# Experts that gather their rows by a table of tokens, in place of a scatter into slots

## The chip, the cores and the metric

The kernel runs on one core of one Trainium2 chip. The time is device time in microseconds of one execution; the kernel before has a median of 3042.47 us. The program is one launch with all of a small decoder in it, and the change touches two of its stages.

## The reference, cut to what matters

The part around the change is a layer with a mixture of experts: 2048 tokens (four batches of 512) of 512 numbers, normalized; a classifier into 64, of which 32 are real experts and 32 are empty; the best 8 for each token; each real expert takes its tokens, at most 256.

```python
logits = xf @ w_cls.T
scores = jax.nn.softmax(logits, axis=-1)
_, topk_idx = jax.lax.top_k(scores + bias[None, :], K)        # K = 8 of 64
w = jnp.take_along_axis(scores, topk_idx, axis=-1)
w = w / (w.sum(-1, keepdims=True) + EPS) * SCALE
...
buf = jnp.zeros((E, CAP, H), xf.dtype).at[ids_s, pos].set(x_exp[order], mode='drop')   # 32 x 256 x 512
gu = jnp.einsum('ech,ehf->ecf', buf, w_gate_up)
g, u = jnp.split(gu, 2, axis=-1)
act = jax.nn.silu(g) * u
y = jnp.einsum('eci,eih->ech', act, w_down)
```

`buf` is what the change is about: the rows of each expert, in the order of the tokens (place `pos`), with zeros behind the last.

## The kernel before

The decoder runs in stages, each a function with one program for each engine: attention, `graph_and_router` (names gr_), `experts` (ex_), further attention layers (at_), and a last network (ff_). Between two stages all engines meet at a barrier.

`graph_and_router` works through four batches b. For each, thresholds of a 512x512 matrix are found: ACT and DVE count how many entries are above a test value, POOL works out the next test value (`update(b, r, j)`, L2235 and L2236, in rounds r), and round 8 makes a table of powers of two (L2232). DVE meanwhile strikes out maxima (`strike_out`), builds the adjacency (L2072), adds it to x, normalizes the rows (`normalize`, L2089, which needs `rstds(b, 1)` of POOL, L2240) and does the `router` of the batch: softmax, best 8, `hot` (a one for each choice, L2144), `mask` (L2147), gate weights, and the place of each choice in its expert, which comes from PE's running counts and the sum so far, `taken` (L2172). PE also has "asides": weights of the last network that it turns and mixes, and `late_units`, 16 weight tiles for the attention, of which DVE writes low parts and copies at the end of the stage (L2201, L2204).

The rows of the experts lie in DRAM, in `slot_rows`, 8192 slots of 2 KB. SP zeroes them at the start (L1711, 16 transfers of 1 MB). POOL then sends each token's row to its slots: `scatter(b, lo, hi)` issues indirect DMAs (L2248), one for each tile of 128 tokens and each of the 8 choices, 32 a batch. Their places in POOL's program are written out by hand: those of batches 0 and 1 lie between the rounds of later batches (`EARLY`, `LATE`), those of batches 2 and 3 behind the last round.

`experts` goes through 32 experts with two buffers for everything (u = e % 2). SP loads the 256 rows of an expert (L2353, 512 KB) as soon as PE has turned those of two experts before; PE turns them (L2408), then gate and up, then down of the expert before (L59 to L61: each product is three, of high and low parts). ACT makes the high parts, DVE the low ones (L2493), and POOL the low part of the down weights, `split_d` (L2538), which waits for ACT's high part (L2464). SP loads the weights of the next but one (L2358, L2359). PE's order is turn(k), gate_up(k-1), down(k-2), turn(k+1).

## Time and profile before

| what | us |
|---|---|
| median of 3 runs | 3042.47 |
| lowest and highest | 3036.84, 3046.91 |
| the profiled execution, its own time | 3039.41 |
| its span in the profile | 3037.4 |
| busy in the span: PE, DVE, ACT, POOL | 2468.5, 1837.5, 1242.0, 855.3 |
| graph_and_router | about 668 to 1162 |
| experts | 1162 to about 1471 |

All times in the profile count from the start of the span. A row of the timeline has the start, the duration, the engine, the line, the operation and tiles, and in brackets how long the engine had been idle and what it waited for. "issue" is idle time for which the profile shows no releaser. "DMA to landing" counts from the start of the issuing instruction. The granted clock is a share of 2.4 GHz.

### The profile page before, as it was taken

How to read it: one execution, taken by the hardware profiler on the slowest of the kernel's cores; microseconds unless marked ns; L12 is line 12 of the kernel's file. 1: busy time of each engine (PE TensorE's matmuls, PEld its weight loads, DVE VectorE, ACT ScalarE, POOL GpSimd, SP SyncE). 2: the span in 40 equal slices, each digit the busy share in tenths (PEclk: the TensorE clock that was granted, in tenths of full speed). 3: DMA queues.
4: the chain of work that ended last, by engine and by line, in shares of the span. 5: the costliest groups of instructions: out<-in, count | busy, mean ns of one | idle time of the engine just before them, and what ended most of it. 6: DMA issues, size and time to landing. Idle time of an engine off the chain costs nothing. (4 is left out here: it accounts for less than half of the span.)

```text
span 3037.4 us, 34907 instructions
## 1 busy us (share of the span) xinstructions
PE 2468.5 (81%) x12662; PEld 1636.9 (54%) x12662; DVE 1837.5 (60%) x2917; ACT 1242.0 (41%) x1873; POOL 855.3 (28%) x1198
## 2 busy tenths in 40 slices
PE   5898989863443356999448999999999869999999
PEld 4454545321221135999334554545555538888887
DVE  3766576627888964777557777565655544444443
ACT  2444444328656624666203433344333323333332
POOL 2232222215578773333443332001211110000000
PEclk8999999976665677999768999999999979999999
DMA  3213131227122245999585656333433323101000
GB/s 117 64 43 84 43 84 46 70 77 287 62 97 92 84 161 180 305 304 303 173 182 138 157 147 156 88 89 100 113 95 92 102 85 133 42 1 42 1 28 14
DMA packets 200952, 340.40 MB, mean 112 GB/s; under 512 B 28809, under 2 KB 60425, under 8 KB 198754
## 3 DMA queue, kind: packets, MB, share of 16 engines
q1 hardware_dynamic: 177250, 299.80, 32.5%
q0 software_dynamic: 20480, 37.87, 5.1%
q8 instruction: 86, 1.41, 0.2%
q10 hardware_dynamic: 3072, 0.79, 0.1%
q14 instruction: 64, 0.52, 0.1%
HBM read 182.30 MB, written 109.05 MB: 96 GB/s over the span
## 5 line engine op out<-in xcount | busy, mean ns | idle before, releaser
L757 DVE TENSOR_REDUCE at_negmax<-at_ps 128x2 f32<-128x1024 f32 (+3 forms) x256 | 259.1, 1016 | 120.7 <-PE at_ps L523 63.7
L670 ACT ACTIVATE at_probs<-at_ps 128x1024 f32<-128x1024 f32 (+3 forms) x256 | 221.7, 866 | 269.9 <-PE at_ps L538 267.6
L1367 DVE TENSOR_REDUCE a_negmax<-a_ps 128x2 f32<-128x1024 f32 x128 | 155.1, 1217 | 137.0 <-PE a_ps L1120 136.4
L1896 ACT ACTIVATE gr_act_signs<-gr_signed,gr_test 128x512 bf16<-128x512 f32 x248 | 177.2, 716 | 81.5 <-POOL gr_test L2236 53.4
L59 PE MATMUL ff_ps<-ff_xnT_hi,ff_s_hi 128*128 128x512 f32 x512 | 201.1, 393 | 5.1 <-DVE ff_xnT_lo L2766 5.1
L61 PE MATMUL ff_ps<-ff_xnT_hi,ff_s_lo 128*128 128x512 f32 x512 | 200.4, 391 | 0.0
L60 PE MATMUL ff_ps<-ff_xnT_lo,ff_s_hi 128*128 128x512 f32 x512 | 200.4, 391 | 0.0
L538 PE MATMUL at_ps<-at_qk 98*128 98x512 f32 (+3 forms) x512 | 172.1, 418 | 21.2 <-DMA at_qk<-at_mrow 11.5
L2796 DVE TENSOR_TENSOR ff_hid<-ff_hid,ff_ps 128x512 f32<-128x512 f32 x64 | 44.0, 688 | 238.6 <-ACT ff_hid L2741 238.6
L1268 ACT ACTIVATE a_probs<-a_ps 128x1024 f32<-128x1024 f32 x128 | 130.9, 1023 | 135.1 <-PE a_ps L1138 134.6
L518 PE MATMUL at_ps<-at_qk 96*128 96x512 f32 (+3 forms) x512 | 162.4, 381 | 19.5 <-DVE at_xnT_lo L818 8.9
L538 PEld LDWEIGHTS at_ps<-at_qk 98*128 98x128 f32 x512 | 83.2, 194 | 163.2 <-issue 91.9
L2741 ACT ACTIVATE ff_hid<-ff_ps 128x512 f32<-128x512 f32 x64 | 38.3, 598 | 303.4 <-PE ff_ps L61 303.4
L2538 POOL TENSOR_TENSOR ex_d_lo<-first_d,ex_d_hi 128x1024 fp32r<-128x1024 f32 x32 | 95.9, 2996 | 216.1 <-ACT ex_d_hi L2464 216.1
L59 PE MATMUL ex_ps<-ex_x_hi,ex_gu_hi 128*128 128x256 f32 x512 | 148.0, 289 | 0.0
L2248 POOL DMA_INDIRECT slot_rows<-shared_x,slots x128 | 135.6, 1060 | 40.1 <-issue 40.1
L60 PE MATMUL ex_ps<-ex_x_lo,ex_gu_hi 128*128 128x256 f32 x512 | 145.3, 284 | 0.0
L61 PE MATMUL ex_ps<-ex_x_hi,ex_gu_lo 128*128 128x256 f32 x512 | 145.3, 284 | 0.0
L852 POOL TENSOR_SCALAR_AFFINE_SELECT at_probs<-at_probs 128x256 f32<-128x256 f32 x128 | 52.4, 410 | 292.1 <-ACT at_probs L670 292.1
L782 DVE RECIPROCAL at_weighed<-at_weighed 128x128 f32<-128x128 f32 x128 | 119.8, 940 | 15.1 <-ACT at_weighed L705 15.1
L726 ACT CAST at_part<-at_ps 128x512 fp32r<-128x512 f32 x64 | 37.4, 587 | 215.8 <-PE at_ps L61 204.2
L873 POOL TENSOR_TENSOR at_oT<-at_weighed 128x512 f32<-128x512 f32 x32 | 40.7, 1272 | 298.0 <-DVE at_weighed L782 298.0
(410 smaller groups left out, 6557.1 us busy)
## 6 DMA issues: line engine op xcount, KB each, us to landing
at_qk<-at_part SPq DMA_DIRECT2D x384, 128.0 KB, 2.5
first_gu<-in_L_ffn_w_gate_up_dram SPq DMA_DIRECT2D x32, 1024.0 KB, 5.6
a_qk<-a_part SPq DMA_DIRECT2D x192, 128.0 KB, 2.3
slot_rows<-gr_zeros SPq DMA_DIRECT2D x16, 1024.0 KB
first_d<-in_L_ffn_w_down_dram SPq DMA_DIRECT2D x32, 512.0 KB, 6.5
ex_rows<-slot_rows SPq DMA_DIRECT2D x32, 512.0 KB, 4.6
out_rows<-ex_y SPq DMA_DIRECT2D x32, 512.0 KB, 3.1
gr_aside_raw<-in_L_ffn_W_dram SPq DMA_DIRECT2D x48, 256.0 KB, 3.1
```

Source lines behind the costliest of these rows:

```text
L59: pe.matmul(out, lh, rh, start=start, stop=False, skip_group_check=True)
L60: pe.matmul(out, lh, rl, start=False, stop=False, skip_group_check=True)
L61: return pe.matmul(out, ll, rh, start=False, stop=stop, skip_group_check=True)
L518: mm = pe.matmul(bank(key, i, 0, n), qk[0:KROWS, g % STACKS, 0, j, t * P:(t + 1) * P], qk[0:KROWS, g % STACKS, 1, j, 0:n], start=True, sto ...
L538: mm = pe.matmul(bank(key, i, lo), qk[0:KROWS + 2, g % STACKS, 1, j, t * P:(t + 1) * P], qk[0:KROWS + 2, g % STACKS, 0, j, lo:S], start=Tr ...
L670: act.activation(probs[:, t % 2, 2 * w:2 * w + 2, lo:S], banks(("kq", g, s), lo), ACT.Exp, scale=SCALE).then_inc(free(("kq", g, s)), 1)
L757: dve.reduce_max(negmax[:, g % 2, :].rearrange("p (j t) -> p j t", t=NT)[:, 2 * w:2 * w + 2, t], banks(("qk", g, s), 0, width(g, t)), AX.X ...
L782: dve.reciprocal(weighed[:, 1, t * P:(t + 1) * P], weighed[:, 1, t * P:(t + 1) * P]).then_inc(rec_done, 1)
L1268: act.activation(probs[:, t % 2, 2 * w:2 * w + 2, :], banks(("kq", g, s)), ACT.Exp, scale=SCALE).then_inc(free(("kq", g, s)), 1)
L1367: dve.reduce_max(negmax[:, g % 2, :].rearrange("p (j t) -> p j t", t=NT)[:, 2 * w:2 * w + 2, t], banks(("qk", g, s)), AX.X, negate=True).t ...
L1896: act.activation(act_signs[:, j, :], src, ACT.Sign, scale=-1.0, bias=against, accum_out=total[:, i, j:j + 1]).then_inc(counted_to[j], 1)
L2248: pool.indirect_dma_start(slot_rows, bass.IndirectOffsetOnAxis(slots[:, n:n + 1], 0), xn[:, b % 2, at // TOPK, :], None, bounds_check=SLOT ...
```

## The change

Nothing is scattered and nothing is zeroed but one row. DVE's normalized rows go to DRAM as they are (`normed`, 2049 rows, row 0 all zeros), by one direct DMA of SP for each batch. What is computed is, for each slot, the number of its token (0 for an empty slot): the table `index`, 128 x 64.

The table is made by PE from products of ones. A place from 0 to 255 is taken apart by DVE into a block (of 8) and a row in it (of 32) (`places`). DVE writes `rows_hot`, a one at the row, by one comparison 128x4096 for each batch (`write_rows`). POOL writes `block_hot`, the token's number in its tile and the tile's number at the block (`blocks_hot`, ten operations). PE multiplies the two, 32 matmuls a batch, summed over the 128 tokens (`table`); DVE adds each batch to `found` (`add_table`). At the end `sum_tokens` joins the two numbers, 16 small matmuls move them to the partitions (`move_tokens`) and `keep_index` writes them as integers.

In `experts` SP's row load is gone. POOL gathers: two indirect DMAs of 128 rows for each expert (`gather`). `hot` is bf16 now, and the sum for the gate weights is made in two halves. `rstds(b-1, 1)` of POOL stands behind round 7 for every batch (it was 8 for batch 1 and 5 for the others).

```diff
+        rows_hot, block_hot = sb("rows_hot", [P, NT, E_ROUTED, ROW], BF16), sb("block_hot", [P, 2, NT, E_ROUTED, BLOCKS], BF16)
...
-            many = slot_rows.rearrange("(p q r) d -> q p (r d)", p=P, r=zeros.shape[1] // D)
-            for q in range(ZERO_DMAS):
-                sp.dma_start(many[q], zeros[:]).then_inc(zeroed, 16)
-            sp.dma_start(none_row, zeros[0:1, 0:D]).then_inc(zeroed, 16)
+            for dst in (none_row, normed[0:1, :]):
+                sp.dma_start(dst, zeros[0:1, 0:D]).then_inc(zeroed, 16)
+            normed_tiles = normed[1:T + 1, :].rearrange("(b t p) d -> b p t d", p=P, t=NT)
+
+            def store_normed(b):
+                sp.wait_ge(xn_done, NT * (b + 1))
+                sp.dma_start(normed_tiles[b], xn[:, b % 2]).then_inc(normed_out, 16)
...
+            def table(b):
+                pe.wait_ge(logT_copied, b + 1)
+                pe.wait_ge(blocks_set, b + 1)
+                pe.wait_ge(vector_rows, b + 1)
+                for t in range(NT):
+                    for g in range(GROUPS):
+                        e = SIDE * g
+                        mm = pe.matmul(ps[:, LOGT, g * P // 2:(g + 1) * P // 2], rows_hot[:, t, e:e + SIDE, :].rearrange("p e r -> p (e r)"),
+                                       block_hot[:, :, t, e:e + SIDE, :], start=t + g == 0, stop=t == NT - 1 and g == GROUPS - 1, skip_group_check=True)
+                mm.then_inc(tabled, 1)
+
+            def move_tokens():
+                pe.wait_ge(index_step, 1)
+                by_side = token_of[:].rearrange("p g (t w) -> p w g t", w=SIDE)
+                for h in range(SIDE):
+                    for w in range(SIDE):
+                        mm = pe.matmul(ps[ROW * w:ROW * (w + 1), MOVED, h * GROUPS * HALVES:(h + 1) * GROUPS * HALVES], env.ident[:, ROW * h:ROW * (h + 1)],
+                                       by_side[:, w], start=True, stop=True, skip_group_check=True)
+                mm.then_inc(moved, 1)
...
                 choices(b)
                 run_asides(b + 1)
+                if b + 1 < B:
+                    table(b)
             for u, (j, c) in enumerate(late_units):
+                if u == len(LATE_BANKS):
+                    table(B - 1)
+                    move_tokens()
...
             def normalize(b):
                 dve.wait_ge(rstd_done[1], b + 1)
                 if b >= 2:
-                    dve.wait_ge(scattered[b % 2], 16 * NT * TOPK * (b // 2))
+                    dve.wait_ge(normed_out, 16 * (b - 1))
                 for t in range(NT):
                     dve.tensor_scalar(xn[:, b % 2, t, :], xo[:, t, :], mv[:, 1, t, 0:1], rstd[:, 1, t, 0:1],
                                       ALU.subtract, ALU.mult).then_inc(xn_done, 1)
+
+            def add_table(b):
+                dve.wait_ge(tabled, b + 1)
+                for h in range(SIDE):
+                    here = slice(ROW * h, ROW * (h + 1))
+                    new = ps[here, LOGT, :].rearrange("p (g n h k) -> p h g n k", n=2, h=SIDE, k=BLOCKS)[:, h]
+                    if b:
+                        dve.tensor_tensor(found[here], found[here], new, ALU.add).then_inc(tab_added, 1)
+                    else:
+                        dve.tensor_copy(found[here], new).then_inc(tab_added, 1)
 
             def finish(b):
                 exact_bounds(b)
                 adjacency(b)
                 blend_x(b)
+                if b:
+                    add_table(b - 1)
...
                 def gate_weights():
-                    for t in range(NT):
-                        step(dve.tensor_tensor(prod[:, t], hot[:, t], bcast_mid(score[:, t, :], TOPK), ALU.mult), wait=t == NT - 1)
-                    step(dve.reduce_sum(k8[:, 0, :], prod[:].rearrange("p t k e -> p (t k) e"), AX.X))
+                    for u in range(2):
+                        for i in range(2):
+                            t = 2 * u + i
+                            step(dve.tensor_tensor(prod[:, i], hot[:, t], bcast_mid(score[:, t, :], TOPK), ALU.mult), wait=i == 1)
+                        step(dve.reduce_sum(k8[:, 0, 2 * u * TOPK:2 * (u + 1) * TOPK], prod[:].rearrange("p t k e -> p (t k) e"), AX.X))
...
+                def places():
                     dve.wait_ge(counted, b + 1)
                     step(dve.tensor_tensor(place[:], counts[:, 0:NT * E_ROUTED].rearrange("p (t e) -> p t e", e=E_ROUTED),
                                            bcast_mid(taken[:], NT), ALU.add))
                     step(dve.tensor_tensor(taken[:], taken[:], counts[:, NT * E_ROUTED:(NT + 1) * E_ROUTED], ALU.add))
+                    if b:
+                        dve.wait_ge(blocks_set, b)
+                    flat, chosen = place[:].rearrange("p t e -> p (t e)"), mask[:].rearrange("p t e -> p (t e)")
+                    dve.tensor_scalar(row[:], flat, 1.0 / ROW, 0.5 / ROW - 0.5, ALU.mult, ALU.add).then_inc(decoding, 1)
+                    dve.wait_ge(decoding, DECODE * b + 1)
+                    dve.tensor_scalar(block_of[:], row[:], 1.5 * 2.0 ** 23, 1.5 * 2.0 ** 23, ALU.add, ALU.subtract).then_inc(decoding, 1)
+                    dve.wait_ge(decoding, DECODE * b + 2)
+                    dve.scalar_tensor_tensor(out=row[:], in0=block_of[:], scalar=-float(ROW), in1=flat, op0=ALU.mult, op1=ALU.add).then_inc(decoding, 1)
+                    dve.wait_ge(decoding, DECODE * b + 3)
+                    dve.scalar_tensor_tensor(out=row[:], in0=row[:], scalar=1.0, in1=chosen, op0=ALU.add, op1=ALU.mult).then_inc(decoding, 1)
...
+            def write_rows(b):
+                dve.wait_ge(decoding, DECODE * (b + 1))
+                dve.wait_ge(numbers_set, 1)
+                if b:
+                    dve.wait_ge(tabled, b)
+                dve.tensor_tensor(rows_hot[:].rearrange("p t e r -> p (t e) r"), bcast_mid(row_iota[:], NT * E_ROUTED),
+                                  bcast_last(row[:], NT * E_ROUTED, ROW), ALU.is_equal).then_inc(vector_rows, 1)
+
+            def sum_tokens():
+                add_table(B - 1)
+                dve.wait_ge(tab_added, SIDE * B)
+                dve.scalar_tensor_tensor(out=token_of[:], in0=found[:, :, 1, :], scalar=float(P), in1=found[:, :, 0, :], op0=ALU.mult, op1=ALU.add
+                                         ).then_inc(index_step, 1)
+
+            def keep_index():
+                dve.wait_ge(moved, 1)
+                dve.tensor_copy(index[:], ps[:, MOVED, 0:SLOTS // P]).then_inc(index_kept, 1)
 
             strike_out(0, 0, ROUNDS + 1)
             for b in range(B):
                 finish(b)
             for u, (j, c) in enumerate(late_units):
                 high, low = late_jobs[j][1:]
+                if u == len(LATE_BANKS):
+                    sum_tokens()
+                if u == 2 * len(LATE_BANKS):
+                    keep_index()
...
-            def scatter(b, lo, hi):
-                for at in range(lo, hi):
-                    if at == 0:
-                        pool.wait_ge(slots_done, 2 * b + 1)
-                        pool.tensor_tensor(pool_carrier[:, b:b + 1], env.minus_half[:, 0:1], env.minus_half[:, 0:1], ALU.mult)
-                    n = b * NT * TOPK + at
-                    pool.indirect_dma_start(slot_rows, bass.IndirectOffsetOnAxis(slots[:, n:n + 1], 0), xn[:, b % 2, at // TOPK, :], None,
-                                            bounds_check=SLOTS - 1, oob_is_err=False).then_inc(scattered[b % 2], 16)
+            def blocks_hot(b):
+                pool.wait_ge(decoding, DECODE * (b + 1))
+                if b:
+                    pool.wait_ge(tabled, b)
+                for n in range(BLOCKS):
+                    pool.tensor_scalar(in_block.rearrange("p (e k) -> p e k", k=BLOCKS)[:, :, n], block_of[:], float(n), None, ALU.is_equal).then_inc(numbers, 1)
+                pool.wait_ge(numbers, (BLOCKS + 1) * b + BLOCKS)
+                pool.tensor_tensor(block_hot[:, 1].rearrange("p t e k -> p t (e k)"), in_block.rearrange("p (t m) -> p t m", t=NT),
+                                   bcast_last(tile_no[:, NT * b:NT * (b + 1)], NT, E_ROUTED * BLOCKS), ALU.mult).then_inc(numbers, 1)
+                pool.wait_ge(numbers, (BLOCKS + 1) * (b + 1))
+                pool.tensor_scalar(in_block, in_block, token[:, 0:1], None, ALU.mult).then_inc(blocks_set, 1)
...
-            LATE = 22
-            EARLY = {0: 2, 4: 5, 5: 1, 7: 1, 9: 3, 10: 1, 11: 2, 13: 2, 15: 1, 17: 1, 18: 1, 20: 1, 21: 1}
-            assert sum(EARLY.values()) + TESTS - LATE == NT * TOPK
             for b in range(B):
-                sent = TESTS - LATE
                 for r in range(TESTS):
                     for j in range(COUNTED[b]):
                         update(b, r, j)
-                    if b and r == (8 if b == 1 else 5):
+                    if b and r == 7:
                         rstds(b - 1, 1)
-                    if b >= 2 and r in EARLY:
-                        scatter(b - 2, sent, sent + EARLY[r])
-                        sent += EARLY[r]
-                    if 0 < b < B - 1 and r >= LATE:
-                        if b == 1 and r == LATE:
-                            pool.wait_ge(zeroed, 16 * (ZERO_DMAS + 1))
-                        scatter(b - 1, r - LATE, r - LATE + 1)
+                if b:
+                    blocks_hot(b - 1)
                 rstds(b, 0)
-            scatter(B - 2, 0, 12)
             rstds(B - 1, 1)
-            scatter(B - 2, 12, NT * TOPK)
-            scatter(B - 1, 0, NT * TOPK)
-            for i in range(2):
-                pool.wait_ge(scattered[i], 16 * NT * TOPK * B // 2)
-
+            blocks_hot(B - 1)
...
-                turned[u].wait(sp, i, 0)
-                sp.dma_start(rows[:, u], rows_dram[bass.ds(e, 1)].rearrange("e p t d -> (e p) t d")).then_inc(rows_in[u].sem, 16)
...
+            def gather(e):
+                i, u = e // 2, e % 2
+                turned[u].wait(pool, i, 0)
+                for t in range(CT):
+                    at = CT * (E_ROUTED // SIDE * (e % SIDE) + e // SIDE) + t
+                    pool.indirect_dma_start(rows[:, u, t, :], None, normed, bass.IndirectOffsetOnAxis(index[:, at:at + 1], 0)).then_inc(rows_in[u].sem, 16)
+
+            gather(0)
+            gather(1)
             split_d(0, 0)
             split_d(0, 1)
+            gather(2)
             for e in range(E_ROUTED):
+                if e + 3 < E_ROUTED:
+                    gather(e + 3)
                 if e + 2 < E_ROUTED:
                     split_d(e // 2 + 1, e % 2)
```

The order of the instructions shows three places. The names of semaphores in brackets are those of an earlier stage that had the same numbers; the sentences say what they stand for here.

POOL at the end of the graph stage, before. The last rounds are behind it; a0_norm_done stands for the slots of a batch, a0_feat_done and a0_kf_ready for DVE's statistics.

```order
L2240 TENSOR_TENSOR gr_rstd<-gr_mv,minus_half 128x4 [waits a0_feat_done]
L2246 TENSOR_TENSOR gr_pool_carrier<-minus_half 128x1 [waits a0_norm_done]
L2248 DMA slot_rows<-shared_x,slots 8192x512 x12
L2240 TENSOR_TENSOR gr_rstd<-gr_mv,minus_half 128x4 [waits a0_kf_ready]
L2248 DMA slot_rows<-shared_x,slots 8192x512 x20
L2246 TENSOR_TENSOR gr_pool_carrier<-minus_half 128x1 [waits a0_norm_done]
L2248 DMA slot_rows<-shared_x,slots 8192x512 x32
```

The same place now: a0_y_ready stands for the decoded places of the batch.

```order
L2349 TENSOR_SCALAR gr_block_hot<-gr_block_of 128x128 x7
L2351 TENSOR_TENSOR gr_block_hot<-gr_block_hot,gr_tile_no 128x1024 [waits gr_numbers]
L2354 TENSOR_SCALAR gr_block_hot<-gr_block_hot,gr_token 128x1024 [waits gr_numbers]
L2342 TENSOR_TENSOR gr_rstd<-gr_mv,minus_half 128x4 [waits a0_feat_done]
L2342 TENSOR_TENSOR gr_rstd<-gr_mv,minus_half 128x4 [waits a0_kf_ready]
L2349 TENSOR_SCALAR gr_block_hot<-gr_block_of 128x128 [waits gr_tabled,a0_y_ready]
```

The 64 scatters that stood here are gone, and each batch's ten operations stand in front of a rstd of the next, or last.

POOL in the experts, before: only the splits, each waiting for ACT's high part (a0_ones_set for the even experts, a0_rows_set for the odd).

```order
L2538 TENSOR_TENSOR ex_d_lo<-first_d,ex_d_hi 128x1024 [waits a0_ones_set]
L2538 TENSOR_TENSOR ex_d_lo<-first_d,ex_d_hi 128x1024 [waits a0_rows_set]
L2538 TENSOR_TENSOR ex_d_lo<-first_d,ex_d_hi 128x1024 [waits a0_ones_set]
L2538 TENSOR_TENSOR ex_d_lo<-first_d,ex_d_hi 128x1024 [waits a0_rows_set]
L2538 TENSOR_TENSOR ex_d_lo<-first_d,ex_d_hi 128x1024 [waits a0_ones_set]
```

And now, from the split of expert 0 on (a0_xT_hi and a0_p_ready stand for PE's turn of the even and the odd experts).

```order
L2634 TENSOR_TENSOR ex_d_lo<-first_d,ex_d_hi 128x1024 [waits a0_ones_set]
L2634 TENSOR_TENSOR ex_d_lo<-first_d,ex_d_hi 128x1024 [waits a0_rows_set]
L2644 DMA ex_rows<-normed,index 128x512 [waits a0_xT_hi]
L2644 DMA ex_rows<-normed,index 128x512
L2644 DMA ex_rows<-normed,index 128x512 [waits a0_p_ready]
L2644 DMA ex_rows<-normed,index 128x512
L2634 TENSOR_TENSOR ex_d_lo<-first_d,ex_d_hi 128x1024 [waits a0_ones_set]
L2644 DMA ex_rows<-normed,index 128x512 [waits a0_xT_hi]
L2644 DMA ex_rows<-normed,index 128x512
L2634 TENSOR_TENSOR ex_d_lo<-first_d,ex_d_hi 128x1024 [waits a0_rows_set]
```

From gather(4) on the order is split, gather, split, gather: split_d(j) stands in front of gather(j+2).

DVE at the end of the graph stage, now. Before, the late weights (L2204 and L2201 of before) followed each other here; a0_sums_out is DVE's own last result.

```order
L2269 TENSOR_TENSOR weights<-gr_k 128x32 [waits a0_sums_out]
L2306 TENSOR_TENSOR at_wq_lo<-gr_ps,at_wq_hi 128x512 [waits gr_late_high] x4
L2147 TENSOR_TENSOR gr_found<-gr_found,gr_ps 32x128 [waits gr_tabled]
L2147 TENSOR_TENSOR gr_found<-gr_found,gr_ps 32x128 x3
L2284 SCALAR_TENSOR_TENSOR gr_token_of<-gr_found 128x64 [waits gr_tab_added]
L2306 TENSOR_TENSOR at_wk_lo<-gr_ps,at_wk_hi 128x512 [waits gr_late_high] x4
L2289 CAST index<-gr_ps 128x64 [waits gr_moved]
L2306 TENSOR_TENSOR at_wv_lo<-gr_ps,at_wv_hi 128x512 [waits gr_late_high] x4
L2303 COPY at_wo<-gr_ps 128x512 [waits gr_late_turned] x4
```

The additions wait for PE's last table, and the index for PE's moves, with the late weights of three more matrices queued behind.

## Rows read from the trace of the kernel before

**Rows 1.** windows of three stretches: us, busy time, granted clock, DMA share

```profile
core 0: us, PE busy (x) PEld busy (x) DVE busy (x) ACT busy (x) POOL busy (x), PEclk, DMA share, GB/s
668.00:1067.00 399.00, 150.31 (x500) 82.87 (x501) 330.71 (x963) 255.76 (x638) 260.61 (x645) 0.64 0.37 129
1067.00:1162.00 95.00, 39.12 (x188) 26.49 (x186) 45.13 (x112) 17.45 (x31) 67.78 (x68) 0.68 0.39 128
1200.00:1440.00 240.00, 238.42 (x1725) 223.16 (x1724) 179.04 (x153) 156.78 (x166) 75.18 (x26) 1.00 0.90 302
```

**Rows 2.** timeline at the boundary: start us, duration, engine, line, wait

```profile
1067.57 1.10 POOL L2248 DMA_INDIRECT slot_rows<-shared_x,slots  x1 [0.17 <-issue]
...
1153.63 0.97 POOL L2248 DMA_INDIRECT slot_rows<-shared_x,slots  x1 [0.30 <-issue]
1124.90 2.47 DVE L2201 COPY at_wo<-gr_ps 128x512 f32<-128x512 f32 x4
1161.97 0.88 SPq L2353 DMA_DIRECT2D ex_rows<-slot_rows  x2
1165.53 1.97 PE L2408 MATMUL ex_ps<-ident,ex_rows 128*128 128x128 f32 x8 [39.84 <-DMA ex_rows<-slot_rows]
```

**Rows 3.** timeline of DVE in the graph stage, rows with a wait

```profile
792.27 1.92 DVE L2089 TENSOR_SCALAR shared_x<-shared_rows,gr_mv,gr_rstd 128x512 f32<-128x512 f32 x4 [7.98 <-POOL gr_rstd L2240]
906.63 0.42 DVE L2126 TENSOR_REDUCE gr_r<-gr_ps 128x4 f32<-128x256 f32 x1 [2.21 <-PE gr_ps L1794]
967.00 0.74 DVE L2051 TENSOR_SCALAR_CACHE_REDUCE gr_dve_flags<-gr_signed,gr_test 128x512 bf16<-128x512 f32 x1 [4.84 <-POOL gr_test L2236]
1017.04 0.42 DVE L2130 TENSOR_REDUCE gr_r<-gr_expd 128x4 f32<-128x256 f32 x1 [2.60 <-ACT gr_expd L1909]
```

**Rows 4.** timeline of SP, PE and POOL, early in the graph stage

```profile
676.11 17.62 SPq L1711 DMA_DIRECT2D slot_rows<-gr_zeros  x14
723.42 1.09 PE L1823 MATMUL gr_ps<-ident,gr_aside_raw 128*128 128x128 f32 x4 [5.43 <-DMA gr_aside_raw<-in_L_ffn_W_dram]
788.60 0.29 POOL L2229 TENSOR_SCALAR gr_half<-gr_total,gr_offset 128x1 f32<-128x1 f32 x1 [0.19 <-ACT gr_act_signs L1896]
791.19 1.05 POOL L2240 TENSOR_TENSOR gr_rstd<-gr_mv,minus_half 128x4 f32<-128x4 f32 x1
```

**Rows 5.** groups of 668 to 1162, each shape apart

```profile
L2144 DVE TENSOR_TENSOR gr_hot<-gr_iota,gr_choice 128x2048 f32<-128x2048 f32 x4 | 9.2, 2294 | 0.1
L2147 DVE TENSOR_REDUCE gr_mask<-gr_hot 128x128 bf16<-128x1024 f32 x4 | 7.6, 1888 | 0.1
L2172 DVE TENSOR_TENSOR gr_place<-gr_ps,gr_taken 128x128 f32<-128x128 f32 x4 | 1.2, 291 | 0.6 <-PE gr_ps L1806 0.5
L2232 POOL TENSOR_SCALAR gr_steps<-gr_powers,gr_base 128x23 f32<-128x23 f32 x8 | 3.0, 380 | 0.0
```

**Rows 6.** timeline of POOL and DVE at 815 us

```profile
815.12 2.38 POOL L2235 TENSOR_SCALAR gr_half<-gr_total,gr_offset 128x1 f32<-128x1 f32 x1
815.05 2.29 DVE L2144 TENSOR_TENSOR gr_hot<-gr_iota,gr_choice 128x2048 f32<-128x2048 f32 x1
```

**Rows 7.** timeline of one period of the experts

```profile
1301.07 1.03 PE L2408 MATMUL ex_ps<-ident,ex_rows 128*128 128x128 f32 x8
1310.45 1.03 PE L2408 MATMUL ex_ps<-ident,ex_rows 128*128 128x128 f32 x8
1302.39 2.97 POOL L2538 TENSOR_TENSOR ex_d_lo<-first_d,ex_d_hi 128x1024 fp32r<-128x1024 f32 x1 [6.41 <-ACT ex_d_hi L2464]
1307.09 2.29 DVE L2493 TENSOR_TENSOR ex_gu_lo<-first_gu,ex_gu_hi 128x2048 fp32r<-128x2048 f32 x1
```

**Rows 8.** operations of L270, the gathers of the attention

```profile
L270 POOL DMA_INDIRECT shared_rows<-out_rows,slots x102: 940/964/1474, 1524.7 to 1871.2; - x102
DMA to landing us min/median/max: 3.8/5.4/9.4
```

**Rows 9.** operations of L2353, the experts' row loads, 1180 to 1450

```profile
DMA to landing us min/median/max: 4.3/4.7/8.0
```

85 lines of the change are left out of this document (59 added, 26 removed).

## The prediction, made before the changed kernel had run

> **What bounds the kernel now.** I read the windows by stage first [rows 1]. The graph stage (668 to 1162 us) has PE busy for only 189 of 494 us, DVE for 331 of 399 us before 1067 us; this stage waits for DVE and the engines that hand it numbers. In the experts (1200 to 1440) PE is busy 238.42 of 240 us at full clock, the DMA engines 0.90 of the time: nothing there is free on PE's side, and whatever makes PE wait is paid in full. Then the boundary between the two, engine by engine [rows 2]. DVE ends its last late weight at 1124.90 + 2.47 = 1127.4. POOL goes on issuing scatters, 64 of them from 1067.57 to 1153.63, one in (1153.63 - 1067.57) / 63 = 1.37 us, and SP starts the experts' first load at 1161.97, 34.6 us after DVE was done. So POOL's queue of scatters sets this boundary. Third, DVE's own waits inside the stage [rows 3]: on POOL's rstd (7.98) and test (4.84), on PE's logits (2.21) and ACT's exponentials (2.60).
>
> **The change, part by part.** The sum is made against the profiled execution (3039.41 us, span 3037.4).
>
> Zeroing slot_rows goes. SP issues it from 676.11 for 17.6 us and more [rows 4], 16 MB through the engines that the first asides need: PE waits 5.43 us there for a raw tile [rows 4]. The loop runs 1.5 to 2 us late by it at DVE. **-1.7**. For batch 1, rstds(0, 1) moves from behind round 8 of POOL's loop to behind round 7. Round 8 is the costly one, with the powers: from 788.60 to the rstd at 791.19 [rows 4], 2.6 us. DVE waits 7.98 us for this rstd [rows 3], so it gains **-2.7**. For batches 2 and 3 it moves from round 5 to 7. A round of the rest of the loop takes 2 to 3 us; these batches' normalize then waits longer for POOL, by my reading of the rounds in all **+3.1** (bounds: 0, if POOL is ahead by then, and two rounds for each, +10).
>
> VectorE's work per batch. places() is four operations 128x128; the nearest row is the one that adds `taken`, 291 ns [rows 5], so with gaps 1.3 us. write_rows compares 128x4096; the same comparison at 128x2048 takes 2294 ns [rows 5], so 4.4 to 4.6. The output is bf16 and no longer f32; I take no gain for it (at half the time it would be 2.3 and the routers 9 us shorter together). Splitting the sum over `prod` in two adds 0.3. Together 6.0 to 6.1 in every router. The bf16 `hot` may make the mask's sum (1888 ns [rows 5]) shorter; I take 0.25 a batch, 1.0 in all.
>
> What of that shows. Batch 0: all, **+6.1**. Batch 1: the router's waits for PE (2.21) and ACT (2.60), and then the one for POOL's test (4.84) [rows 3], come from queues that this DVE work doesn't move, so a later DVE waits less, and the batch gains what POOL, without scatters between its rounds, is earlier: 6.0 - 9.7 = **-3.7**. Batch 2: the first two kinds alone, at about the same size, 6.0 - 4.6 = **+1.4**. The bound on the other side is that those waits move along with DVE: 9.7 + 4.6 more. add_table, four copies from PSUM over 32 partitions, 0.25 to 0.3 each: **+1.1** once; the others lie in a wait. Up to the last adjacency: -1.7 - 2.7 + 3.1 + 6.1 - 3.7 + 1.1 + 1.4 = **+3.6**; with the mask's gain +2.6.
>
> POOL in the stage. It loses 128 scatters (1.37 us of its queue each, above) and gains blocks_hot four times: eight 128x128 operations and two of 128x1024. The nearest POOL rows are 380 ns for 128x23 [rows 5] and 2.97 for 128x1024 with two SBUF inputs [rows 7]; with one it should be under that, so 8 x 0.3 + 2 x 2.5 = 7.4 us. It stands behind the rounds, and then the next rstds(b, 0) and PE's table. As POOL idles for ACT there, 7.4 is mostly cover; if the cover is gone, three times 3 us are paid, which I keep for the range. PE's 32 table matmuls a batch stand behind its asides, in a stage in which PE is idle more than half of the time [rows 1]; I cost them at nothing.
>
> The end of the stage. After: DVE ends at 1127.4 + 6.1 (last router) + 1.5 (add_table, token_of) + 3.5 to 4 (it must see POOL's last blocks_hot, the last table and the 16 f32 moves) + 0.3 (index) = 1139.0 to 1139.4. Between the last work of the stage and SP's first issue of the next lies the engines' barrier: after the last scatter's end, 1154.60, it was 7.4 us with that scatter's landing [rows 2]. Here nothing is in the air, and I take 1.2 (bounds 0 and 7.4). So the experts begin at 1140.6, not 1161.97: **-21.2**. Ahead of the experts: 2.6 - 21.2 = **-18.6**.
>
> Experts, first one. From SP's issue to PE's turn there were 1161.97 to 1165.53 [rows 2], 3.6. Now POOL issues two gathers and the second must land: 1.27 + 5.4 = 6.7. **+3**.
>
> Experts, steady. Here the order matters: POOL does split_d(j), gather(j+2), split_d(j+1), gather(j+3). One turn at 1301.07, next at 1310.45, 9.38 later [rows 7]. POOL's split_d runs from 1302.39 to 1305.36 [rows 7], 4.29 behind the turn, and it is split_d(14) behind turn 15; so gather(16) stands behind it and has to have landed by turn 16. Gathers take 0.96 us each [rows 8], and "issue", 0.3, stands between two DMAs of POOL [rows 2]: the second is issued from 5.87 to 6.84 behind the turn, and 9.38 - 5.87 = 3.5 us are left for landing (measured from the start of the issue). Before, SP's load was free from 1.4 on, with 8 us left for a 4.7 landing [rows 9]. The gathers that the trace has, of the same shape from DRAM to SBUF in the attention, land in 3.8 / 5.4 / 9.4 (least, median, most) [rows 8]: more than 3.5 even at the least. POOL waits for ACT's copy of the weights, and that for PE's down ahead of the turn; so a late turn isn't passed on by one expert but by two. With period p and landing L: 2p = 5.87 + 9.38 + L, and PE stalls (L - 3.5) / 2 per expert. L = 3.8 gives 0.15, 5.4 gives 0.95, 6.5 gives 1.5.
>
> To that comes DVE. While it runs a large operation with two SBUF inputs POOL's own doesn't proceed: an operation of 0.35 us took 2.38 beside the 2.29 of L2144, and ended with it [rows 6]. The experts' gu_lo is such an operation, from 1307.09 for 2.29 us [rows 7], 6.02 behind the turn, right on the second gather. In the other parity it starts 1.3 later. So the second gather ends up to 1.5 us later in half of the experts: on average 0.6 of chain, 0.3 of stall. Stall 0.95 + 0.3 = 1.25 us, for 29 experts **+36**.
>
> The Trainium skill has a rule for the lock (SBUF — State Buffer: the port pair that DVE and GpSimd share is held for a full instruction by a DVE operation with two SBUF inputs, against a GpSimd one that reads SBUF). The trace agrees, by the 2.38 us above. By that page alone every second gather that meets gu_lo would wait for its end, at 8.31 behind the turn.
>
> Sum: -18.6 + 3 + 36 = **+20** on 3039.4, 3060. The median of the runs shown is 3042.5, 3 above the profiled one; I give **3062**. Costed at nothing: store_normed, four direct stores of 1 MB in place of 32 MB of scatters, under a DMA share of 0.37 [rows 1]; if one were in the way it would be by some 3 us.
>
> **Rivals.**
> (a) No stall: faster. The gathers land within 3.5 us, or POOL gets ahead of PE. Then -18.6 + 3 = -15.6: 3025 to 3030. It decides from a landing of 3.9, where 29 x 0.2 eats 6 of the 15.6 and 9 are left. For it: the scatters were a cheap transfer, issued every 1.37 us with no wait but "issue" [rows 2]. Against it: no gather of the trace landed under 3.8, and in the experts other transfers hold the engines for 0.90 of the time [rows 1].
> The Trainium skill speaks for this one (DMA: Bandwidth & Descriptors, on the anatomy of a software-generated DMA): 2.0 us plus the bytes at 436 GB/s, an estimate of 2.6 us for 256 KB. By that there would be no stall and 3027. The trace disagrees with it, 3.8 at the least and 5.4 in the median.
> (b) A heavy stall: the gathers share the engines with 1.5 MB of weights, which SP issues as split_d ends, so at the same moment. The upper part of the spread, 6.5 to 9.4, would give 1.5 to 2.9, with gu_lo 1.8 to 3.2: +52 to +90, so 3078 to 3115. For it: the share of 0.90, and the simultaneous issue. Against it: the rows load of today is as large, in the same share, and landed in 4.7 [rows 9].
> (c) They cancel: landing 4 to 5, stall 0.2 to 0.85 with the lock, 3033 to 3052.
> (d) The graph stage gives nothing: blocks_hot or the table isn't covered and the last one delays the index by 7 us more; PE's granted clock, 0.64 to 0.68 on the mean of this stage [rows 1], between its levels of 0.5 (1.2 GHz) and 1.0 (2.4 GHz), stays longer on the lower one. That adds 5 to 15 to any of the others.
>
> **How the numbers follow.** My forecast, a stall of 0.9 to 1.6, has 0.42 (own range 3050 to 3078). (a) 0.17, (b) 0.16, (c) 0.25, with (d) spread over them. Low end: between (a) and (c) 3028; high: the landing of 7 with the lock, 3092. That leaves about 0.1 on each side. 0.3%, 9.1 us, is what a measurement of this kernel can tell from no change: faster is (a) and a little of (c), 0.2; same most of (c), 0.2; slower 0.6.
>
> **What would show it.** In the profile after: the first gather near 1141; nothing named slot_rows; DVE's comparison 128x4096 near 4.5 us; PE's turn in the experts with a wait on the rows' DMA of about 1.2 us each, and a period of 10.6 and not 9.38; the gathers' landing median near 5.4; PE's clock still full in the experts; ends of the second gather stretched beside gu_lo. Wrong would be: turns without a wait (then (a)); a first gather after 1150 (then (d)); or waits that PE shows on d_lo in place of the rows, which would say that POOL's queue itself, and not the landing, is late.

## The result and the profile after

The changed kernel takes 3102.07 us in the median (3097.72 to 3104.90, 4 runs), the kernel before 3041.34 beside it (3036.84 to 3046.91, 4 runs): a ratio of 1.0198, with a 95% interval of 1.0176 to 1.0219. It is slower by about 60 us, where 20 were forecast, and outside the range (3028 to 3092). The profiled execution has 3097.72 us, 58.3 more than that of before.

The windows of the changed kernel, with the boundary of the stages where it lies now, answer to [rows 1].

```profile
core 0: us, PE busy (x) PEld busy (x) DVE busy (x) ACT busy (x) POOL busy (x), PEclk, DMA share, GB/s
668.00:1067.00 399.00, 157.03 (x576) 88.97 (x576) 344.04 (x974) 257.95 (x642) 237.97 (x614) 0.61 0.28 90
1067.00:1146.00 79.00, 38.02 (x270) 28.97 (x270) 60.14 (x144) 14.41 (x26) 21.47 (x13) 0.74 0.39 142
1200.00:1440.00 240.00, 206.31 (x1371) 192.56 (x1371) 141.94 (x121) 124.21 (x130) 99.64 (x60) 0.93 0.70 239
```

In the experts PE is busy 206 of 240 us, where it was 238, and the mean clock is 0.93 and not 1.00. The DMA share fell from 0.90 to 0.70: the engines had less to do in the same time, so they are no bound by themselves. A stage that was full has got holes.

Cut at the same places in both profiles, the time went like this. The stage starts at DVE's first instruction of it, 668.92 before and 672.65 after.

| piece | before | after | difference | forecast |
|---|---|---|---|---|
| start of the graph stage to the adjacency of batch 3 | 401.4 | 402.7 | +1.3 | +2.6 |
| from there to the first issue of the experts' rows | 91.6 | 71.0 | -20.6 | -21.2 |
| issue to the first turn of PE | 3.6 | 5.4 | +1.9 | +3 |
| first turn to the 32nd | 287.4 | 363.4 | +76.0 | +36 |
| all that the change doesn't touch (ahead of and behind it) | 2253.4 | 2253.4 | 0 | 0 |

The 0 of the last row hides two differences of the same size: the stage starts 3.7 us later, and the time behind the last turn is 3.8 us shorter (1580.7 us and not 1584.5). They cancel by chance, and nothing here says why they differ. The row "start of the graph stage to the adjacency" rests on one profile of each kernel. Of the nine other profiles of versions that leave this stretch alone six have 402.4 to 402.7 us there, and three 405.0 to 405.9.

One term is wrong, by 40 us. The boundary, in the timeline after (to be held against [rows 2]):

```profile
1111.64 11.96 POOL L2349 TENSOR_SCALAR gr_block_hot<-gr_block_of 128x128 bf16<-128x128 f32 x8 [21.66 <-DVE gr_row L2247]
1126.12 2.85 POOL L2354 TENSOR_SCALAR gr_block_hot<-gr_block_hot,gr_token 128x1024 bf16<-128x1024 bf16 x1
1129.07 1.87 PE L1855 MATMUL gr_ps<-gr_block_hot,gr_rows_hot 128*128 128x64 bf16 x32 [8.55 <-issue]
1141.69 2.47 DVE L2303 COPY at_wo<-gr_ps 128x512 f32<-128x512 f32 x4
1146.38 1.26 POOL L2644 DMA_INDIRECT ex_rows<-normed,index  x1 [17.41 <-SPq L180]
1151.82 1.97 PE L2504 MATMUL ex_ps<-ident,ex_rows 128*128 128x128 f32 x8 [9.33 <-DMA ex_rows<-normed,index]
```

POOL gathers from 1146.38 (at 1161.97 SP loaded before, in a profile that had begun the stage 3.7 us earlier). The last ones of blocks_hot run from 1111.64 to 1128.97, 17.3 us for which I had put 7.4. PE has been idle for 8.55 us when its table starts, 0.1 us behind them (the row names no releaser), but DVE's router ends only at 1129.4, so most of it was hidden.

DVE in the graph stage, timeline, against [rows 3], with the first and the last row by which the pieces were cut:

```profile
672.65 0.09 DVE L2026 MEMSET gr_taken<- 128x32 f32 x1 [3.26 <-PEq L53]
790.82 1.92 DVE L2138 TENSOR_SCALAR shared_x<-shared_rows,gr_mv,gr_rstd 128x512 f32<-128x512 f32 x4 [4.44 <-POOL gr_rstd L2342]
895.80 1.92 DVE L2138 TENSOR_SCALAR shared_x<-shared_rows,gr_mv,gr_rstd 128x512 f32<-128x512 f32 x4 [3.88 <-POOL gr_rstd L2342]
1075.34 2.49 DVE L2121 SCALAR_TENSOR_TENSOR gr_adjacent<-gr_adjacent,first_gu 128x512 f32<-128x512 f32 x4
```

And the groups of the stage, DVE and POOL, each shape apart (line, operation, shapes, count, busy us, mean ns, idle before):

```profile
L2278 DVE TENSOR_TENSOR gr_rows_hot<-gr_row_iota,gr_row 128x4096 bf16<-128x4096 f32 x4 | 17.7, 4425 | 0.1
L2187 DVE TENSOR_REDUCE gr_r<-gr_ps 128x4 f32<-128x256 f32 x4 | 1.7, 421 | 8.4 <-PE gr_ps L1816 8.2
L2191 DVE TENSOR_REDUCE gr_r<-gr_expd 128x4 f32<-128x256 f32 x4 | 1.7, 417 | 0.7 <-ACT gr_expd L1958 0.6
L2208 DVE TENSOR_REDUCE gr_mask<-gr_hot 128x128 bf16<-128x1024 bf16 x4 | 7.5, 1881 | 0.1
L2349 POOL TENSOR_SCALAR gr_block_hot<-gr_block_of 128x128 bf16<-128x128 f32 x32 | 32.1, 1153 | 22.9 <-DVE gr_row L2247 21.7
```

The wait for batch 0's rstd fell from 7.98 us [rows 3] to 4.44, and that for batch 1's rose from 2.10 to 3.88. The waits for PE's logits are 8.4 us summed over the four batches, of which 8.23 stand in the last one (8.39 before), and those for the exponentials are 0.7: the waits of batches 1 and 2 that I had expected to be eaten are eaten.

One period of two experts in the timeline, against [rows 7], and the last turn:

```profile
1228.72 1.03 PE L2504 MATMUL ex_ps<-ident,ex_rows 128*128 128x128 f32 x8
1230.04 2.97 POOL L2634 TENSOR_TENSOR ex_d_lo<-first_d,ex_d_hi 128x1024 fp32r<-128x1024 f32 x1 [9.21 <-ACT ex_d_hi L2560]
1233.16 1.24 POOL L2644 DMA_INDIRECT ex_rows<-normed,index  x1
1234.70 0.95 POOL L2644 DMA_INDIRECT ex_rows<-normed,index  x1 [0.30 <-issue]
1234.74 2.29 DVE L2589 TENSOR_TENSOR ex_gu_lo<-first_gu,ex_gu_hi 128x2048 fp32r<-128x2048 f32 x1
1241.63 1.92 PE L2504 MATMUL ex_ps<-ident,ex_rows 128*128 128x128 f32 x8 [3.38 <-DMA ex_rows<-normed,index]
1252.63 1.03 PE L2504 MATMUL ex_ps<-ident,ex_rows 128*128 128x128 f32 x8
...
1515.20 1.03 PE L2504 MATMUL ex_ps<-ident,ex_rows 128*128 128x128 f32 x8
```

The turn at 1228.72 has no wait. Behind it POOL splits, issues one gather and then the second, at 1234.70, 5.98 behind the turn. PE is done 9.5 us behind that turn and waits 3.38 us more for the rows; 1241.63 - 1234.70 = 6.9 us from the issue to PE's start. The next turn has no wait, and lies 11.00 us on, not 9.38. What the operations of L2644 (the gathers) say together:

```profile
L2644 POOL DMA_INDIRECT ex_rows<-normed,index x64: 945/950/1991, 1146.4 to 1506.4; - x64
  PE ex_ps L2504: 61.2, 16
DMA to landing us min/median/max: 3.4/6.7/8.2
```

61.2 us of waits of PE in 16 places, 9.33 of them at the very first. A landing of 6.7 in the median, where I had taken 5.4. So 51.9 of the 76.0 us are waits. The other 24 are in the turns' distance after each wait: 15 times 11.00 - 9.38 = 1.6. The windows behind the wait that ends at 1241.6, columns as above, show in what:

```profile
1241.60:1244.60 3.00, 2.97 (x14) 2.97 (x15) 1.06 (x2) 1.63 (x3) 2.54 (x3) 0.52 1.08 300
1244.60:1247.60 3.00, 3.00 (x25) 3.00 (x24) 2.39 (x2) 1.80 (x2) 0.09 (x1) 0.91 1.11 359
1247.60:1250.60 3.00, 3.00 (x25) 2.87 (x24) 1.13 (x1) 0.00 (x0) 0.00 (x0) 1.00 1.03 372
```

The granted clock is 0.52 for the first 3 us behind a wait of 3.4 us, then 0.91, then 1.00. PE is busy all through them. At 0.5 (1.2 GHz) it does half as much: (1 - 0.52) x 3 + (1 - 0.91) x 3 = 1.7 us lost.

### The profile page after: what moved, and what is told of

It reads as the page before. It is cut to its first block and busy times, and to the rows that moved or that the text cites. A ratio compares the mean times of both kernels' runs of the same rounds, so it can differ in the third digit from the quotient of the medians.

```text
span 3095.9 us, 35090 instructions
## 1 busy us (share of the span) xinstructions
PE 2499.3 (81%) x12822; PEld 1665.5 (54%) x12822; DVE 1864.9 (60%) x2959; ACT 1241.8 (40%) x1873; POOL 851.1 (27%) x1176
## 5 line engine op out<-in xcount | busy, mean ns | idle before, releaser
L59 PE MATMUL ex_ps<-ex_x_hi,ex_gu_hi 128*128 128x256 f32 x512 | 155.1, 303 | 0.0
L630 PE MATMUL at_ps<-at_wo,at_oT 128*128 128x512 f32 x256 | 115.8, 606 | 6.8 <-POOL at_oT L873 6.6
```

Source lines behind the costliest of these rows:

```text
L59: pe.matmul(out, lh, rh, start=start, stop=False, skip_group_check=True)
L630: mm = pe.matmul(bank(key, i), oT[:, dc, t * P:(t + 1) * P], woT[:, dc, :], start=dc == 0, stop=dc == NC - 1, skip_group_check=True)
```

## The experiments

**The gathers ahead of the split.** One change of order in POOL's program:

```diff
             split_d(0, 0)
-            split_d(0, 1)
             gather(2)
+            split_d(0, 1)
+            gather(3)
             for e in range(E_ROUTED):
-                if e + 3 < E_ROUTED:
-                    gather(e + 3)
+                if e + 4 < E_ROUTED:
+                    gather(e + 4)
```

> POOL's order in the experts is changed: gather(k+2) stands in front of split_d(k), so that it waits only for the turn of expert k. Theory A (the gather's place behind the split is late, and its landing of 6.7 us does not fit into the 3.5 us that are left): the gather is issued near the turn two experts ahead and has over 14 us to land, so PE's waits of 3.3 us at every other turn are gone, the period is 9.38 again, 32 turns take about 288 us and not 363, the clock is full, and the time is about 3098 - 76 = 3022. Theory B (the engines of the DMA are the limit, or gathers are slow for what goes on beside them, so that an earlier issue only makes them wait longer): turns still wait 2 to 3 us, and the time stays above 3080.

Measured: 3032.13 us (10 runs) beside 3040.73 of before, ratio 0.9972 (0.9960 to 0.9984). The landing is still slow, 7.0 us in the median and 9.9 at most, and nobody waits for it but the first turn. Theory B falls: with the same transfers beside them, gathers that are issued one expert earlier are in time. The 32 turns take 292.2 us; 288 were expected, and 3022. What the rest is shows in the windows of its experts, first and second half (columns as above):

```profile
1200.00:1317.00 117.00, 117.00 (x845) 109.95 (x844) 86.51 (x74) 75.97 (x81) 61.72 (x38) 1.00 0.89 306
1317.00:1447.00 130.00, 125.58 (x891) 115.79 (x890) 109.80 (x79) 81.06 (x86) 64.23 (x37) 1.00 0.86 289
```

In the first half PE is busy all the time, at full clock. In the second, the periods of the last 13 turns are 9.68 to 10.48 us and not 9.38, and DVE's busy time rises from 0.74 to 0.84 of the stretch, without more to do. The timeline there, POOL and DVE:

```profile
1397.71 2.40 POOL L2634 TENSOR_TENSOR ex_d_lo<-first_d,ex_d_hi 128x1024 fp32r<-128x1024 f32 x1 [4.14 <-ACT ex_d_hi L2560]
1398.30 2.89 DVE L2621 TENSOR_TENSOR shared_x<-shared_x 128x1024 f32<-128x1024 f32 x1
```

The butterfly of DVE (L2621, 128x1024, two operands in SBUF), 1.22 us in the first half, takes 2.89: it ends 1.1 us behind POOL's split, which had begun 0.6 us before it. The split is as short as it ever was (2.40). Before the change the butterfly was first, and the split, 0.5 us behind it, took 2.97 [rows 7]:

```profile
1301.87 1.22 DVE L2525 TENSOR_TENSOR shared_x<-shared_x 128x1024 f32<-128x1024 f32 x1
```

So whoever starts first of the two holds up the other. ACT had waited 2.07 us for a weight load until 1313.8, and that made DVE late once; by my reading each late butterfly (2.81 to 3.36 us, to the end) then kept DVE late for the next. When this version was run again, it went the same way: a wait of ACT for the weights until 1344.9 (2.35 us), and from the next butterfly on 2.82 to 3.36 us each.

**The rows by a direct load of SP**, with the new graph stage. The gathers are left out, and SP loads where it did before, from another array, so the experts compute on other rows.

```diff
                 e = i * 2 + u
+                turned[u].wait(sp, i, 0)
+                sp.dma_start(rows[:, u], gu_dram[bass.ds(e, 1)].rearrange("e p c f -> (e p) c f")[:, 0:CT, :]).then_inc(rows_in[u].sem, 16)
```

> No gather: SP loads 512 KB for each expert as before the change, by one direct DMA where it stood, from another array (the first half of each expert's gate and up weights), so the experts compute on other rows than the reference's. The table is made as in the changed kernel. It isolates what the graph stage gives. Theory A: experts as before the change (287 us), so the time is 3040 - 19 (the stage, by the two profiles) = about 3021, and the version with the gathers ahead is within 5 us of it. Theory B: about 3021 here too, but the version with the gathers ahead far above it.

Measured: 3020.34, ratio 0.9939 (0.9920 to 0.9958), and 287.6 us for the 32 turns. The 20.4 us are the value of the new graph stage alone, for which the sum had 18.6. The version with the gathers ahead is 12 us above it, not within 5, of which its profile has 4.5 in the experts and 5.3 in a later start of the graph stage, ahead of all that the two kernels differ in.

**PE kept busy in front of the wait.**

```diff
-                rows_in[u].wait(pe, i, 16 * CT)
                 if after is not None:
                     x_lo_done[after[1]].wait(pe, after[0], 1)
+                for _ in range(WARM if u == 0 else 0):
+                    pe.matmul(ps[:, 0, 0:P], env.ident[:], env.ident[:], start=True, stop=True)
+                rows_in[u].wait(pe, i, 16 * CT)
```

> The changed kernel with 26 extra matmuls of 128x128 on PE (about 3.3 us at full clock) in front of its wait for the rows of every even expert; their result is overwritten. The profile shows 11.0 us from the even expert's turn to the odd one's with no wait in them, 1.6 more than 9.38, while the mean clock of the experts is 0.93. Theory C (the waits cost more than their length, since the clock is lower behind each): with PE busy through the wait the clock stays full, 15 times 1.6 = 24 us are saved although PE does more, and the time is about 3075. Theory D (the 1.6 us are something else, such as late weights or parts from DVE or ACT): no saving, 3100 or more.

Measured: 3109.04, ratio 1.0219. As a time it is a miss, since 26 of these matmuls take 5.8 us and not 3.3, more than the wait they cover. But from the even turn to the odd one it is 9.38 us in every full pair but one (9.44), where it was 11.0, and the clock of the whole stretch is 1.00. With 14 of them:

> The changed kernel with 14 extra matmuls in front of the wait of every even expert; the 26 of the first try took 5.8 us (0.22 each) and not 3.3, so they were longer than the wait, and all turns were at full clock and 9.38 us from even to odd. 14 should take 3.1 us. Theory C (the lower clock behind a wait costs 1.6 us every time): a pair of experts takes 18.76 + 3.3 = 22.1 us and not 23.9, and the time is 15 x 1.8 = 27 us below the changed kernel's, 3075. Theory D: no gain over 3102.

Measured: 3074.77, ratio 1.0063 (1.0046 to 1.0080). The 32 turns take 339.0 us and not 363.4, 24.4 less (27 were expected), with 15 times 3.3 us more work on PE. Eight turns still wait for their rows, 9.5 us together. The whole time isn't set against the 3102 of the changed kernel, since this group of runs was slower: its kernel before had 3055.51. One pair (the row of L2502 is the added work; the last is a window):

```profile
1253.31 3.29 PE L2502 MATMUL ex_ps<-ident 128*128 128x128 f32 x28
1256.44 1.04 PE L2507 MATMUL ex_ps<-ident,ex_rows 128*128 128x128 f32 x8
1266.02 1.06 PE L2507 MATMUL ex_ps<-ident,ex_rows 128*128 128x128 f32 x8
1256.40:1265.80 9.40, 9.40 (x70) 8.74 (x69) 4.90 (x4) 3.98 (x5) 3.07 (x3) 1.00 0.67 232
```

The turn is 1.04 us long again behind the added work, where it was 1.92, and the clock is 1.00. Theory D falls: the 1.6 us per pair are the clock's price for the wait.

**The weights cut** from 1.5 MB to 64 KB for each expert:

```diff
-                sp.dma_start(raw_gu[:, u], gu_dram[bass.ds(e, 1)].rearrange("e p c f -> (e p) c f")).then_inc(w_in[u].sem, 16)
+                sp.dma_start(raw_gu[:, u, 0, 0:64], gu_dram[bass.ds(e, 1)].rearrange("e p c f -> (e p) c f")[:, 0, 0:64]).then_inc(w_in[u].sem, 16)
...
```

(The down weights are cut in the same way.)

> The changed kernel with SP's weight loads of the experts cut from 1.5 MB to 64 KB each (64 columns of the gate and up weights and 64 of the down weights; the rest of the buffers keeps older values, so the output is not the reference's). If the gathers' landing of 6.7 us comes from sharing the DMA engines with the weights, it falls to 4 to 5 us, the waits of PE to (L - 3.5), 0.5 to 1.5 at every other turn, and the time to about 3045. If the gathers are slow by themselves, the landing stays at 6 to 7 and so do the waits.

Measured: 3043.82 (one run). Operations of the gathers again, who waited and the landing:

```profile
  PE ex_ps L2504: 25.8, 16
DMA to landing us min/median/max: 3.3/4.2/6.4
```

The landing falls from 6.7 to 4.2, and PE's waits to mostly 0.9 us at every other turn, of which I had said 0.5 to 1.5. (4.2 - 3.5 is 0.7.) So 2.5 of the 6.7 us are the weights, which SP issues within 1.6 us of the gathers (at 1233.08 and 1233.50 in the period that the result shows). The trace of this run shows one thing more: behind waits of 0.87 to 0.91 us the next turn comes 9.43 or 9.44 us on, so waits as short as these did not have the price that those of 3.4 us had.

**A direct load at the late moment.** SP's load again, but behind SP's own wait for split_d, right in front of the weights:

```diff
                 turned[u].wait(sp, i, 0)
+                if weights:
+                    gu_lo_done[u].wait(sp, i, 0)
+                    d_lo_done[u].wait(sp, i, 0)
                 sp.dma_start(rows[:, u], ...).then_inc(rows_in[u].sem, 16)
```

> The kernel with SP's direct load of the rows (from another array, so the output is not the reference's), but the load is issued only after SP's wait for split_d, right in front of the weights: 4.3 us behind the turn, with 5.0 us left to land. If it is the moment, together with 1.5 MB of weights, that makes a landing of 4.7 to one of 6 to 7, the direct load waits too: 1 to 2 us at every other turn and a time of 3040 to 3055. If only gathers are slow, it lands in under 5 and the time stays near 3021.

Measured: 3024.41 (one run), 291.2 us for the 32 turns. Its row loads, 1180 to 1430, and its window:

```profile
DMA to landing us min/median/max: 3.7/3.9/7.1
1200.00:1440.00 240.00, 236.20 (x1698) 221.22 (x1697) 174.29 (x150) 154.72 (x162) 73.99 (x25) 0.99 0.87 298
```

The direct load at its early place, for comparison, in the second experiment:

```profile
DMA to landing us min/median/max: 4.2/5.0/8.4
```

The forecast of 1 to 2 us of waits at every other turn was wrong: four turns wait, 3.8 us together (four and 1.5 us in the kernel before). Behind the longest of them, 2.01 us, the next turn comes 10.99 us on; behind the one of 0.94 us it comes 9.44 on. The direct load lands in 3.9 us, faster than at its early place (5.0), though 1.5 MB of weights follow 0.4 us behind. A late moment is not enough; it takes the gather as well. The gather is issued in two parts, the second 1.5 us later, on another queue, when the weights are already in the engines. Which of these (the queue, the second issue, the single rows) costs how much wasn't tried apart.

**The butterfly moved.** On top of the gathers ahead:

```diff
+                butterfly(2 * i + u)
                 y_ready[u].wait(dve, i, 2)
                 y_out[u].wait(dve, i, 0)
                 dve.tensor_copy(y[:, u, 1, :], ps[:, 7, :]).then_inc(y_dve[u].sem, 1)
```

> The version with the gathers ahead, and DVE's butterfly on the weights of a later stage (128x1024, two SBUF inputs) moved in front of its copy of y, where DVE was idle for 1.26 us, so that it ends before POOL's split_d starts. Theory E (from expert 19 on the profile of the version ahead has periods of 9.9 to 10.1 us, since a late weight load put DVE behind POOL: the split then starts first and the butterfly takes 3.1 us beside it and not 1.22, which keeps DVE late): no butterfly over 1.5 us, all periods 9.4 to 9.5, 32 turns about 288 us and not 292, and a time 4 to 8 us lower than that of the version ahead, about 3025. Theory F (the longer periods come from the DMA engines, 0.89 busy, that the weights wait for): the periods stay near 9.9 and the time at 3032.

Measured: 3028.05, ratio 0.9908 (0.9889 to 0.9928), 286.9 us for the 32 turns. DVE and POOL in its timeline:

```profile
1258.19 1.22 DVE L2622 TENSOR_TENSOR shared_x<-shared_rows 128x1024 f32<-128x1024 f32 x1
1259.43 2.41 POOL L2634 TENSOR_TENSOR ex_d_lo<-first_d,ex_d_hi 128x1024 fp32r<-128x1024 f32 x1 [4.64 <-ACT ex_d_hi L2560]
```

The butterfly ends as the split begins, and both have their short durations, 1.22 and 2.41. The forecast of no butterfly over 1.5 us was missed once: ACT waited 2.97 us for a weight load until 1358.9, the next butterfly took 3.42, and two periods were 10.75 and 10.09. Then they were back at 9.37 to 9.39, where the version before it, once late, stayed late. The late weight load is still there, and what it no longer does is to keep DVE late. Theory F falls.

**The end of the graph stage.**

```diff
+                if u == 2 * len(LATE_BANKS):
                     move_tokens()
...
-                if u == 2 * len(LATE_BANKS):
+                if u == 3 * len(LATE_BANKS):
                     keep_index()
...
-                    if b and r == 7:
+                    if b and r == (7 if b == 1 else 5):
```

> As the one before, and in the graph stage: POOL's rstd of batches 1 and 2 behind round 5 again (round 7 in the change, which my sum priced at +3.1), PE turns late weights 4 to 7 before it moves the tokens, and DVE keeps the index four units later, which would take away a wait of 2.39 us of DVE for ACT. If both prices are right: 4 to 5 us below the kernel before it in this call. If the rstd's place is worth nothing (DVE waited 3.88 for it and 2.10 before, but later waits take that back): 1.5 to 2.5 us.

Measured: 3012.78, ratio 0.9867 (0.9851 to 0.9884). The kernel before had 3055.51 us in this group of runs and 3040.73 in the first, on another chip, so ratios across the groups don't compare. So the three versions (gathers ahead, the butterfly moved too, the stage's end too) were run again together, five rounds each.

> The version with the gathers ahead once more, on one chip with the two that follow, since the kernel before was 15 us slower in the second group of runs than in the first, so that ratios of the two groups can't be set against each other. By the profiles (start of the graph stage to the last turn 771.6 against 784.0 before the change): ratio 0.995 to 0.998. If the ratio of the second group was no accident, 0.993 or less.

> With the butterfly moved as well. By its experts (286.9 us and not 292.2) 5 us under the version ahead, ratio 0.994 to 0.996. If the move does more than the profile shows, as the ratio 0.9908 of the second group would have it, 15 us or more under it.

> With the stage's end and the rstd as well. The profile had the first turn at 471.8 us from the start of the stage, and 479 to 481 without: 7 to 9 us under the one before, ratio 0.991 to 0.993. If it is only the 4 to 5 that I priced: 0.993 to 0.995.

| kernel | us | ratio | 95% interval |
|---|---|---|---|
| before, beside them | 3041.37 | 1 | |
| gathers ahead | 3029.16 | 0.9956 | 0.9941 to 0.9970 |
| and the butterfly moved | 3020.77 | 0.9924 | 0.9910 to 0.9937 |
| and the stage's end | 3016.79 | 0.9913 | 0.9900 to 0.9927 |

The first step is worth 8.4 us in the medians (5 forecast, 3.7 in the experts of these two profiles: 290.3 and 286.6; no profile shows where the rest is). The second is 4.0 in the medians, with intervals that overlap. Its profile has the first turn 472.3 us from the start of the stage and not 479.2, 7.0 us: 3.1 by the rstd (adjacency of batch 3 at 399.5 and not 402.6; the sum had priced its place at 3.1), 3.9 by the end. The 15 us between the two in the earlier group were mostly not the edit.

## Why the prediction was wrong

**Bounds and boundary: right.** POOL's scatters held the experts back, and without them the stage's end came 20.6 us earlier (21.2). That POOL's last blocks_hot took 17.3 us and not 7.4 changed little. (The sum has two slips here: DVE's terms add up to 1138.8 to 1139.3, and from 1161.97 to 1140.6 it is 21.4. They are worth 0.2 us.)

**The graph stage: right in its parts.** write_rows took 4425 ns (4.4 to 4.6). The mask's sum gained nothing from bf16, 1881 ns against 1888; I had taken 1.0 us. By intervals between adjacencies the differences are -1.3, +2.1, -1.7 and +2.2, together +1.3.

**The mechanism of the stall: right.** The recurrence says that a late turn shortens the next wait, so that waits need only fulfil s + s' = L - 3.5. The runs show it in the form 3.4, 0, 3.4, 0. With the landing 6.9 of the second gather it gives 3.4 for a pair. The sign that I had named, about 1.2 us at each turn and a period of 10.6, did not come in that form: the waits stand at every other turn. Moving the gather took the waits away, as it must if its place is the reason.

**The step that failed** is "Stall 0.95 + 0.3 = 1.25 us, for 29 experts +36", in two ways. The landing was taken from the attention's gathers, 5.4, and was 6.7 among the weights' 1.5 MB (4.2 without them). My range had 6.5 to 9.4 in rival (b), which is what came, at 0.16, though I had the simultaneous issue on my list and set against it only the direct load, which the last experiment on it shows to be no guide for a gather. That makes 51.9 us of waits beside the 36. And the clock isn't in the sum at all: I wrote that PE's waits are paid in full, but 3.4 us of idle PE cost 1.6 us on top, 24 us in all. The second way is the one that left the range. With the measured 6.9 and nothing for the lock my own sum gives 29 x 1.7 = 49 us and 3076, inside it; the clock's 24 make it 3100, and 3102 was measured. So it is luck that the time lies in rival (b)'s 3078 to 3115: a landing of 6.7 gives by its terms 3073, with the lock 3082. (Its upper ends are slips too: 9.4 gives about 3120 and not 3115, 7 with the lock 3086 and not 3092.) I priced the clock only for the graph stage, in (d), and named as a sign of success "PE's clock still full in the experts". The rows had what was needed: the granted clock of the graph stage, where PE idles, is 0.64 to 0.68 [rows 1].

**The collision with gu_lo** (0.3 us) cost nothing. The two do meet, in half of the pairs: the second issue starts at 1234.70 and gu_lo at 1234.74. But the gather is first, its issue has the 0.95 us that it has in all pairs, and it lands in 6.6 us (the next one, 1243.74, that gu_lo doesn't meet, in 6.4). Issues that start while such an operation of DVE is already running are stretched: one at the start of the stage, behind gu_lo, to 1.99 us, and the first issue of every second pair to 1.24, behind h_lo (which ends at 1233.56; the issue starts at 1233.16):

```profile
1232.03 1.53 DVE L2589 TENSOR_TENSOR ex_h_lo<-ex_hid,ex_h_hi 128x512 fp32r<-128x512 f32 x1 [0.69 <-ACT ex_h_hi L2570]
1149.32 2.29 DVE L2589 TENSOR_TENSOR ex_gu_lo<-first_gu,ex_gu_hi 128x2048 fp32r<-128x2048 f32 x1 [5.16 <-ACT ex_gu_hi L2556]
1150.44 1.99 POOL L2644 DMA_INDIRECT ex_rows<-normed,index  x1 [0.30 <-issue]
```

Both end 0.82 to 0.84 us behind DVE's operation. So what the term lacked is the order of the two starts, which for gu_lo and the second gather are 0.04 us apart. The collision that counted was another of the same kind, butterfly and split, in a version that I hadn't seen.

**The rivals.** (a) needed a landing under 3.9; the least was 3.4 and the median 6.7. What spoke for it, the cheap scatters, was so, but it did not carry over to gathers. The scatters before, each with as many rows the other way, landed in 2.2 us in the median (L2248):

```profile
DMA to landing us min/median/max: 2.1/2.2/7.0
```

The Trainium skill's fit for a transfer of this size (DMA: Bandwidth & Descriptors, the anatomy of a software-generated DMA) gives 2.6 us, an estimate from that page's figures; the shortest landing of a gather in any run here was 3.3, so the measurement decides against it for a gather. The Trainium skill's rule on the port pair (SBUF — State Buffer, two separate sides, on the shared pair as an exclusive lock) says that whoever starts first holds the pair. That was borne out further than I had used it: the 2.89 us of DVE's butterfly beside a split of 2.40 are that, on DVE's side, and the gathers that started ahead of gu_lo were not held. (c) and (d) did not happen.

## What to carry to other kernels

A DMA that moves from a queue that was free to one behind other work has to be priced from its new place: from when the instruction ahead of it ends to when the data are needed, against the landing in that same traffic, and from its own kind of DMA. Where the margin is short, changing places with the instruction ahead may be enough: here it turned a kernel 2% slower into one 0.3 to 0.4% faster. And in a stage where TensorE runs without a gap, a wait of a few microseconds costs more than its length, since the clock behind it is lower (3.4 us cost 1.6 more here, 0.9 us nothing more); the loss can be tested by filling the wait with idle matmuls, as long as they are not longer than it.
